# Left-over attention rows: their round trip through HBM issued by ScalarE's queue instead of SyncE's

## The reference

```python
x = x + tanh(g_xattn[0]) * xattn(layernorm(x), ctx, Wq, bq, Wkv, bkv, Wo, bo)   # 16 heads of 32, 154 keys
x = x + tanh(g_ffn[0]) * ffn(layernorm(x), w1, b1, w2, b2)                      # 512 -> 2048 -> 512, relu
# ffn: h = relu(x w1' + b1); h and w2 rounded to 4 exponent and 3 mantissa bits; out rounded to float16
```

## Time and profile before

| | us |
|---|---|
| median of 3 runs (lowest, highest) | 1660.89 (1660.31, 1663.74) |
| profiled execution, its own time | 1664.15 |
| span of that execution, first to last instruction | 1662.4 |
| PE busy | 1538.4 (93%) |
| DVE, POOL, ACT busy | 941.5, 864.2, 812.9 |
| mean granted TensorE clock | 0.973 of full speed |

### The profile page before, as it was taken

How to read it: one execution, slowest core, us unless ns; L and a number is a source line. 1 busy time by engine, 2 the same in 40 slices (tenths; PEclk the granted TensorE clock), 3 DMA queues, 4 the chain that set the end, 5 groups by cost and what they waited for, 6 DMA issues and landing times.

```text
span 1662.4 us, 23615 instructions
## 1 busy us (share of the span) xinstructions
PE 1538.4 (93%) x8552; PEld 695.3 (42%) x8552; DVE 941.5 (57%) x1303; ACT 812.9 (49%) x1187; POOL 864.2 (52%) x916
## 2 busy tenths in 40 slices
PE   5765599999989999999989999999989999999998
PEld 3321244444434444444434444444434444444443
DVE  6667546465565656566565746556564655646231
ACT  2355465454535555454625545464535545553511
POOL 1465547364464746465465746465464646545320
PEclk8986899999999999999999999999999999999999
DMA  7243444344442434344352443343343444332110
GB/s 277 61 137 80 112 137 110 112 98 114 77 125 77 114 103 99 108 105 118 72 133 73 105 124 93 104 109 101 90 101 109 99 108 102 90 96 78 48 51 26
DMA packets 249879, 169.30 MB, mean 102 GB/s; under 512 B 165484, under 2 KB 214948, under 8 KB 248100
## 3 DMA queue, kind: packets, MB, share of 16 engines
q1 hardware_dynamic: 247124, 162.08, 37.3%
q10 hardware_dynamic: 2640, 5.72, 0.9%
HBM read 73.36 MB, written 33.55 MB: 64 GB/s over the span
## 4 chain that ended last, share of the span: by engine, by line
PE 56%; DVE 13%; SPq 13%; POOL 6%; issue 5%; DMA 4%; ACT 2%; ACTq 1%; DVEq 0%
PE ring L471 34%; PE ring L643 13%; SPq L354 5%; SPq L331 3%; DVE y L941 3%; PE m_ps L555 2%; DMA resid<-in_x 2%; DVE smax L919 2%; PE s_ps L582 2%; SPq L363 2%; DVE xn L990 2%; DVE resid L981 2%; POOL resid L1086 2%; DVE bns L964 2%; POOL pmain L1054 2%
## 5 line engine op out<-in xcount | busy, mean ns | idle before, releaser
L471 PE MATMUL ring<-late_a,w 128*128 128x512 f16 x3072 | 698.7, 380 | 7.6 <-DMA late_a<-x 7.6
L471 PEld LDWEIGHTS ring<-late_a,w 128*128 128x128 f16 x3072 | 297.8, 98 | 359.7 <-issue 23.8
L1054 POOL TENSOR_TENSOR pmain<-p,pmain 128x512 f16<-128x512 f32 x256 | 304.6, 1192 | 143.2 <-ACT p L727 141.5
L748 ACT ACTIVATE late_b<-ring,b_sb,wsc 128x512 fp8e4<-128x512 f32 x256 | 199.3, 779 | 335.3 <-PE ring L471 335.3
L919 DVE TENSOR_REDUCE smax<-m_ps 128x4 f32<-128x616 f32 x256 | 202.8, 792 | 193.9 <-PE m_ps L555 193.6
L941 DVE RECIPROCAL y<-d_ps 128x256 f32<-128x256 f32 x128 | 224.0, 1750 | 90.6 <-PE d_ps L601 90.6
L727 ACT ACTIVATE p<-s_ps,prob_log,sc 128x512 f32<-128x512 f32 x320 | 247.7, 774 | 0.0
L643 PE MATMUL ring<-w,late_b 128*128 128x512 fp8e4 x1024 | 229.6, 380 | 1.4 <-ACT late_b L748 0.9
L1054 POOL TENSOR_TENSOR pleft<-p,pleft 128x512 f16<-128x512 f32 x64 | 75.1, 1173 | 245.9 <-ACT p L727 245.9
L724 ACT ACTIVATE pmain<-s_ps,prob_log,sc 128x512 f16<-128x512 f32 x256 | 198.0, 774 | 0.9 <-PE s_ps L582 0.9
L471 PE MATMUL ring<-wo,yT 128*128 128x512 f16 x768 | 177.9, 382 | 0.0
(11 more groups left out here) (144 smaller groups left out, 1418.4 us busy)
## 6 DMA issues: line engine op xcount, KB each, us to landing
qstack<-qparts SPq DMA_DIRECT2D x384, 64.0 KB, 2.1
pstack<-left_rows SPq DMA_DIRECT2D x192, 128.0 KB, 2.6
xin<-in_x SPq DMA_DIRECT2D x64, 256.0 KB, 3.2
left_rows<-pleft SPq DMA_DIRECT2D x64, 256.0 KB, 3.1
resid<-in_x SPq DMA_DIRECT2D x64, 256.0 KB, 3.1
out_x<-resid SPq DMA_DIRECT2D x64, 256.0 KB, 2.7
resid<-in_w_t SPq DMA_DIRECT2D x4, 1024.0 KB, 5.2
qstack<-negT SPq DMA_DIRECT2D x128, 2.0 KB, 1.7
```

The costliest lines, as they stand in the source:

```text
L471: last = pe.matmul(dst, lhs(a, k), rhs(b, k), start=(k == 0 and p == 0), stop=(k == n_k - 1 and p == 2))
L748: nc.scalar.activation(hT[:, j, :], ring_bank("h", c, j)[:], ACT.Relu, bias=b1_sb[:, j:j + 1], scale=wsc[:, j // 4, 1:2], saturate=False). ...
L1054: nc.gpsimd.tensor_tensor(part[:, 1, :], p32[:, n % 2, :], part[:, 0, :], ALU.subtract).then_inc(prob_lo, 1)
```

## The change

`left_out` and `left_in` move from SP's program to ACT's. Their waits, tables and DMAs stay as they are. In ACT's beat loop they stand behind `exp_left` and `exp_main` and ahead of everything else of the beat.

```diff
@@ -389,22 +389,6 @@   (@block.sync)
-            def left_out(c, m):
-                g = group(c, m)
-                sp.wait_ge(prob_lo, unit(c, m, 0) + 1)
-                if g >= 2:
-                    sp.wait_ge(left_back, (g - 1) * STACK * DMA)
-                sp.dma_start(left_rows[g % 2], pleft[:]).then_inc(left_away, DMA)
-
-            def left_in(c, m):
-                g = group(c, m)
-                sp.wait_ge(left_away, (g + 1) * DMA)
-                if g:
-                    sp.wait_ge(valued, g)
-                rows = left_rows[g % 2].rearrange("(h k) a n -> a k h n", h=GH)
-                for r in range(STACK):
-                    sp.dma_start(pstack[DH * r:DH * r + DH], rows[r % 2]).then_inc(left_back, DMA)
@@ -448,8 +432,6 @@
                 run(lambda c, t: turn_x(c, t) if c else None, XTURN_AT, beat)
-                run(left_out, LEFT_AWAY_AT, beat)
-                run(left_in, LEFT_BACK_AT, beat)
                 run(reload, RELOAD_AT, beat)
@@ -732,6 +714,22 @@   (@block.scalar: the same two functions, with act in place of sp)
+            def left_out(c, m):
+                g = group(c, m)
+                act.wait_ge(prob_lo, unit(c, m, 0) + 1)
+...
+            def left_in(c, m):
+                g = group(c, m)
+                act.wait_ge(left_away, (g + 1) * DMA)
+...
@@ -795,6 +793,8 @@
                 run(exp_left, LEFT_AT, beat)
                 run(exp_main, MAIN_AT, beat)
+                run(left_out, LEFT_AWAY_AT, beat)
+                run(left_in, LEFT_BACK_AT, beat)
                 run(y_hi, SPLIT_Y_AT, beat)
                 run(x2_hi, LN2_AT, beat)
```

More of the change, by code:

```diff
@@ L733, in exp_left @@
                 exps(c, m, 0, pleft[:, 0, :])
+            def left_out(c, m):
+                g = group(c, m)
+                act.wait_ge(prob_lo, unit(c, m, 0) + 1)
+                if g >= 2:
+                    act.wait_ge(left_back, (g - 1) * STACK * DMA)
+                act.dma_start(left_rows[g % 2], pleft[:]).then_inc(left_away, DMA)
+            def left_in(c, m):
+                g = group(c, m)
+                act.wait_ge(left_away, (g + 1) * DMA)
+                if g:
+                    act.wait_ge(valued, g)
+                rows = left_rows[g % 2].rearrange("(h k) a n -> a k h n", h=GH)
+                for r in range(STACK):
+                    act.dma_start(pstack[DH * r:DH * r + DH], rows[r % 2]).then_inc(left_back, DMA)
             def exp_main(c, k):
```

## The result

The changed kernel takes **1677.5 us** (median of 4 runs, 1672.7 to 1683.6), the kernel before beside it 1661.1 (4 runs, 1660.3 to 1663.7). The ratio is 1.0098, with a 95% interval of 1.0072 to 1.0125: slower by 1%, where I had forecast 1656.6 and at most 1664.5. The profiled execution has a span of 1681.8 us, 19.4 more than before. It is the slowest of the four, 6.1 above their median (the one before was 3.3 above its own), so what is read from its rows comes out a little larger than the 16.4 us of the medians.

A forecast was written before the change was run, and what follows sets the result against it. PE, busy 93% of the span, was taken to bound the kernel, so only its waits could be given back; -5.4 - 0.6 + 0.9 + 0.6 + 0.2 = -4.3 from 1660.89 us gave 1656.6, range 1651 to 1664.5.

The forecast's parts named there:

- The start-up: Before the hidden layer: PE's first `value` no longer waits for the left-over round trip; gains of 5.4 and 0.6 us.
- -5.4: Start-up: earlier `value` lets the third `w1` load and what follows go 5.4 us earlier; bounds 4.4 and 6.1.
- -0.6: End of the start-up: DMA out of group 1 no longer stands ahead of SP's last transposes; 0.6 us gained.
- ACT in an ordinary chunk: Ordinary chunks: relus behind the moved waits and issues do not make PE wait; cost 0, slack 2.3 us.
- SP's speed beside ACT's issues: At the three switches: ACT's issues slow SP's; 0.3 us per switch, 0.9 lost, bounds 0 and 5.6.
- A lock over the whole issue: At the switches: each ACT issue holds SP for its whole length; upper bound of 5.6 us lost.
- The 0.07 per ACT issue: At the switches: SP's slowdown per ACT issue, from twelve SP issues taking 8.48 us beside ACT's, 7.68 alone.
- the 0.6 of the last `w2` load: At the last `w2` load, issued beside a DMA out whose landing may lengthen; 0.6 us lost, bounds 0 and 2.6.
- The 0.2 of the last chunk: Last chunk: PE has no filling work and POOL waits directly for ACT; 0.2 us lost, bounds 0 and 1.4.
- The three switches: At the chunk switches: no gain expected, PE's wait stays, named after POOL, which the late second reload holds.
- slower by the second reload: Rival, chance 0.11: `left_in` in the second reload's beat delays it in 15 chunks; 8.4 us lost, 1665.0.
- The rival's own turning point: Ordinary chunks: the second-reload rival decides from 0.29 us paid per chunk, a reload of 4.3 us.

The follow-up runs named there:

- Run 2: Changed kernel with left-over transfers on ScalarE's (ACT's) queue in chunk 0 alone, on SP's in chunks 1 to 15; 1658.6 us, ratio 0.9971.
- run 3: Changed kernel with the first of four left-over groups back on SP's queue in chunks 1 to 15, the rest on ScalarE's; 1657.8 us, ratio 0.9969.
- run 10: Changed kernel with all reloads issued earlier, 0 and 1 in beat 26, 2 in 28, 3 in 30; 1637.9 us, ratio 0.9849.
- run 13: Kernel before, left-over transfers on SP, with reloads 0 and 1 in beat 26, 2 in 28, 3 in 30; 1650.3 us, ratio 0.9925.

## Why the prediction was wrong

**The start-up was right.** -5.4 and -0.6 were forecast, and the hidden layer's first product is 5.9 us earlier. `value` begins at 84.46 where I said 85.2, the `w1` load at 88.88 where I said 89.5. The times of the issues were not right: they went up to 2.9 us earlier than I said, since I had let them wait for exponentials to start. It cost the sum nothing, for `value` begins when PE is free in any case. In the chain of the changed kernel SP's last transpose of the start-up stands right behind its shift rows, without the DMA out of group 1 between them, which is the 0.6. Run 2, which has chunk 0 alone on ScalarE's queue, holds the 5.4 and not the 0.6: it measures 4.7, within the bounds of 4.4 to 6.1.

**ACT in an ordinary chunk was right.** I put it at 0; its issues took 0.34 and some 0.5 us in the rows above, its relus are waited for by PE no more than before (0.9 us, once), and run 3 with three groups on ScalarE's queue is as fast as run 2.

**SP's speed beside ACT's issues** (0.9 lost) did not show. In the chain of the changed kernel the piece of q that SP issued while ACT issued `left_out` at 638.46 is the one at 638.36, and it took as long as its neighbours:

```profile
637.72 0.60 SPq L354
...
638.36 0.60 SPq L354
...
639.00 0.60 SPq L354
```

ACT's issue of 0.34 us lies wholly inside it. A lock over the whole issue, which the prediction weighed beside the Trainium skill (Perfetto Trace Analysis, section "DMA Instruction — HWDGE (DVE, Sync)"), would have made one of the two longer; these rows don't bear it out. (The section says that the block is locked while it makes the descriptors; that this takes the whole issue was my upper bound, not the section's.) Over the whole span SP's 384 issues for the stack of q have a median of 0.597 us in both kernels. The 0.07 per ACT issue was read from too little: in the kernel before stacks of q with no ACT issue beside them take from 7.68 up to 8.95 us (at 247.42), so the 8.48 needs no ACT issue. For the 0.6 of the last `w2` load nothing shows: it goes out at 229.28, and the DMA out nearest to it, at 227.0, had landed in 2.0 us by then. The 0.2 of the last chunk was not measured apart.

**The three switches were right.** The wait stayed, 6.15, 4.99 and 4.98 us, now named after POOL; for the second of them, at the switch to chunk 8, 4 to 5 was forecast. Its rows:

```profile
842.05 1.26 POOL L1086 TENSOR_TENSOR resid<-resid,gbo 128x512 f32<-128x512 f32 x1 [7.94 <-DMA resid<-in_x]
...
848.12 1.15 POOL L1054 TENSOR_TENSOR pmain<-p,pmain 128x512 f16<-128x512 f32 x1
...
849.33 1.04 PE L580 MATMUL d_ps<-pmain,ones 128*32 128x512 f16 x8 [4.99 <-POOL pmain L1054]
```

That the reload held them is now shown by trial: with early reloads the change frees the switches (run 10 against 13), with the old ones it doesn't. But SP's left-over rows held them too, right behind the reload: with early reloads and the rows on SP's queue the waits stay, 4.52 to 5.58 us (run 13). It takes both changes.

**The step that failed** is the cost of the ordinary chunk. The sum had a term there for ACT's time, 0, and none for the bytes that ACT's queue puts beside SP's. The runs showed a second reload that lands in 4.8 us for 3.1 in ordinary chunks, and 24.3 us lost over twelve chunks of the profiled execution. I had seen the collision and left it to a rival, "slower by the second reload", with a chance of 0.11 and 8.4 us. Its mechanism was the one that decided. Its size was wrong in three ways. It took the landing of chunk 14, 4.54, as the worst case; the row above has 5.45, and the median of the second reload in ordinary chunks is 4.8. It took PE's wait to grow to 1.73; it grew to 2.08. And it left out what a longer wait does to the clock: 12.8 us are slower products, 1.5 to 1.7 us for each of six falls that the kernel before doesn't have, and 3.2 more that I have not followed. The rival's own turning point, a reload of 4.3, was passed. What spoke for giving it a greater chance stood in the same paragraph: 384 KB in the beat of a reload for which POOL already waited 43.8 us in all. I had asked only whether ACT had time for the issues, not what order SP's lateness had given to the two transfers until then. The order, `left_in` 3.8 us behind the reload, was a by-product of a slow queue, and the change took it away.

What stays open: whether the same 384 KB ahead of the reload on SP's own queue, or right behind it on ScalarE's, would delay it as much (order and queue are moved together in these runs); and why a wait of 2.08 us is followed by a fall of the clock in some chunks and not in others (at 664.91, also 2.08, the sixteen products took 3.61). In the chain above the second reload was also issued some 1.2 us late (the stack of q took 8.91 us, where the quickest take 7.7); such slow stacks occur in the kernel before as well, for example 8.49 at 629.66, so I don't put them down to the change.

## What to carry to other kernels

When a transfer is moved to an idle queue, its issue is cheap, but it will start earlier, and on the same DMA engines. Ask which transfer it used to follow, and whether someone already waits for that one; then move that one ahead first. Here the change alone cost 1%. With the reloads in beats 26 to 30 the change takes some 0.75% (12.4 us) off a kernel that these early reloads had already made 0.75% faster, and with the reloads another two beats earlier the two together give 1.9%.

## What the runs showed of the hardware that I had not expected

- A second queue's 384 KB, issued 0.8 to 2.0 us ahead of a 256 KB load, took that load's median landing from 3.1 to 4.8 us; half of it gave 3.3, and another half behind it 5.3 (the second reload in ordinary chunks). On one queue 512 KB directly behind the load left it at 3.0.
- A DMA on ACT's queue was issued at 74.00, 2.3 us ahead of an exponential that stands before it in ACT's program.
- A PE wait of 2.04 to 2.09 us cost up to 1.7 us more than its length, since the next sixteen products ran at a lower granted clock (5.30 for 3.61 us), in 7 of 11 cases. Over the traces of all runs one such fall followed a wait of 1.93 us and one of 2.01, and none a wait before the same products of up to 1.90. A wait longer by 0.9 us (2.08 for 1.17) so cost up to 2.6.
- An issue on ACT's queue of 0.34 us inside one of SP's left that one at 0.60 us.
